# Global attention: values transposed by transposing DMA transfers instead of TensorE transposes and copies

## What is computed

```
def proj(W, bias):
    y = tanh(states @ W + bias)
    return y.reshape(b, s, h, d).transpose(0, 2, 1, 3)
q, k, v = proj(Wq, bq), proj(Wk, bk), proj(Wv, bv)
alpha = einsum('bhqd,bhkd->bhqk', q, k) / sqrt(d)
alpha = softmax(where(causal, alpha, min))
ctx = einsum('bhqk,bhkd->bhqd', alpha, v)
out = tanh(ctx.reshape(b, s, h * d) @ Wo + bo)
```

## Time and profile before

| | us |
|---|---|
| median of 3 runs | 2335.64 (2334.77 to 2335.74) |
| the profiled execution, whole | 2336.77 |
| its span in the profile | 2335.0 |
| PE busy | 2249.1 (96% of the span) |
| DVE busy | 1918.6 (82%) |
| ACT busy | 1510.0 (65%) |
| POOL busy | 525.9 (23%) |
| L785, transposes of values, 512 in all: mean of one | 0.22 |
| L626, copy of the high values, 32 in all: mean of one | 1.02 |
| L338, copy of the low values, 32 in all: mean of one | 0.68 |

### The profile page before, as it was taken

One profiled execution on the slowest core, in us unless ns is written; L12 is line 12 of the kernel. 1 busy time (PEld: TensorE's weight loads), 2 busy tenths in 40 slices (PEclk: granted clock), 3 DMA queues, 4 the chain that ended last, 5 costly groups with the idle time before them and its releaser, 6 DMA issues.

```text
span 2335.0 us, 61234 instructions
## 1 busy us (share of the span) xinstructions
PE 2249.1 (96%) x21120; PEld 1734.1 (74%) x21120; DVE 1918.6 (82%) x4512; ACT 1510.0 (65%) x2969; POOL 525.9 (23%) x637
## 2 busy tenths in 40 slices
PE   6999999999999999889999999999999999998999
PEld 4676777777777767567777777788777777776888
DVE  6999799979998999768888888567588888886776
ACT  5777577757776777447677766444476777765443
POOL 2000000000000000154555554012255555551000
PEclk9999999999999999989999999999999999999999
DMA  3100110001001100210000001000100000001110
GB/s 117 47 13 19 38 40 13 13 31 52 13 13 43 58 13 7 84 58 2 9 0 9 0 9 39 19 1 0 48 1 3 7 4 5 5 5 31 60 36 28
DMA packets 66987, 58.20 MB, mean 25 GB/s; under 512 B 4037, under 2 KB 64317, under 8 KB 66625
## 3 DMA queue, kind: packets, MB, share of 16 engines
q1 hardware_dynamic: 66880, 56.81, 7.9%
HBM read 44.21 MB, written 8.40 MB: 23 GB/s over the span
## 4 chain that ended last, share of the span: by engine, by line
PE 53%; DVE 2%; issue 1%; ACT 1%; POOL 0%; DVEq 0%; POOLq 0%; ACTq 0%
PE ly_ps L74 9%; PE ly_ps L75 9%; PE ly_ps L76 9%; PE ly_ps L1930 6%; PE ly_ps L1909 5%; PE ly_ps L1920 5%; PE ly_ps L1947 5%; PE ly_ps L1901 3%; PE ly_ps L1940 1%; PE ly_ps L1957 1%; PE ly_ps L1985 1%; PE ly_ps L1878 1%; DVE ly_masked L1598 1%; DVE ly_rope_t L1569 0%; DVE ly_rope_a L1566 0%
## 5 line engine op out<-in xcount | busy, mean ns | idle before, releaser
L610 ACT ACTIVATE at_p<-at_ps_s,at_shift 128x1024 f32<-128x1024 f32 (+3 forms) x384 | 335.5, 899 | 89.8 <-PE at_ps_s L814 48.9
L349 DVE TENSOR_TENSOR at_p_lo<-at_p,at_p_hi 128x1024 f16<-128x1024 f32 (+3 forms) x384 | 357.4, 952 | 5.5
L1371 ACT ACTIVATE ly_probs<-ly_masked,ly_small,ly_rq 128x256 f32<-128x256 f32 x512 | 301.6, 594 | 13.8 <-DVE ly_small L1601 13.8
L842 PE MATMUL at_ps_o<-at_v,at_p_hi 128*128 128x65 f16 x2304 | 238.0, 193 | 3.4 <-DVE at_p_lo L349 2.5
L842 PEld LDWEIGHTS at_ps_o<-at_v,at_p_hi 128*128 128x128 f16 x2304 | 210.6, 96 | 38.6 <-issue 25.8
L843 PE MATMUL at_ps_o<-at_v,at_p_hi 128*128 128x64 f16 x2304 | 237.1, 194 | 0.0
L1598 DVE CUSTOM_DVE_ANT_0 ly_masked<-ly_ps,ly_mask 128x256 f32<-128x256 f32 x512 | 196.1, 421 | 49.0 <-PE ly_ps L1909 36.6
L844 PE MATMUL at_ps_o<-at_v,at_p_lo 128*128 128x65 f16 x2304 | 236.0, 192 | 0.0
L1225 POOL TENSOR_TENSOR ly_rope_a<-ly_rope_a,ly_rope_t 128x512 f32<-128x512 f32 x128 | 164.2, 1283 | 318.5 <-DVE ly_rope_t L1569 318.5
L1379 ACT ACTIVATE ly_operands_plain<-ly_ps 128x512 f32<-128x512 f32 x256 | 153.3, 599 | 111.8 <-PE ly_ps L1920 103.9
L344 DVE CAST at_p_hi<-at_p 128x1024 f16<-128x1024 f32 (+3 forms) x384 | 206.8, 557 | 22.3 <-ACT at_p L610 13.5
(11 more groups left out here) (247 smaller groups left out, 6057.6 us busy)
## 6 DMA issues: line engine op xcount, KB each, us to landing
at_w_raw<-in_Wv SPq DMA_DIRECT2D x32, 128.0 KB, 2.3
at_w_raw<-in_Wq SPq DMA_DIRECT2D x32, 128.0 KB, 2.4
at_w_raw<-in_Wk SPq DMA_DIRECT2D x32, 128.0 KB, 2.4
at_xio<-in_states SPq DMA_DIRECT2D x4, 1024.0 KB, 6.7
ly_a_raw<-x SPq DMA_DIRECT2D x8, 512.0 KB, 4.4
out<-stream SPq DMA_DIRECT2D x16, 256.0 KB, 2.3
ly_shifted<-stream SPq DMA_DIRECT2D x8, 508.0 KB
x<-at_xio SPq DMA_DIRECT2D x3, 1024.0 KB, 4.4
```

What stands on the lines that cost most here:

```text
L349: dve.tensor_tensor(p_lo[u % P_RING][:, :, off:], probs[u % P_RING][:, :, off:], p_hi[u % P_RING][:, :, off:], ALU.subtract).then_inc(p_lo ...
L610: act.activation(probs[u % P_RING][:, :, off:], ps_s[u % 2][:, :, off:], ACT.Exp, bias=shift[:], scale=SCORE_SCALE).then_inc(exp_done, 1)
L842: pe.matmul(out, ph, ones_hi, start=(kt == 0 and t == 0), stop=False, skip_group_check=True)
L1371: step = act.activation(pr[:, j % 2, h, :], sm[:, j % 2, h, :], ACT.Exp, bias=small[:, j % 2, 1, h:h + 1], scale=rq[:, par, 2 * j + h:2 * ...
```

## The change

The two parts of `vT` are transposed by three DMA transfers with `transpose=True`, issued by SyncE: one for each head of the high part (64 x 1024), one for the whole low part (128 x 1024). SyncE waits for the second value chunk's low part (`pj_lo`) and issues them behind the weight loads. The value tile is laid out anew: in each tile of 128 keys first the two heads' high values, each with 16 columns of ones behind it (`VS = DH + 16`), then the low values of both. One semaphore, `vt_done`, stands for all three (48 per pair). TensorE's transposes, the copies on ScalarE and VectorE and the waits of the projections 1 to 3 for them go; the first projection of the next pair waits for `vt_done`, since it leads to a write of `vT`, and so do the value products. SyncE's loop over pairs is written out.

```diff
-VW = 2 * DH + 2
+VS = DH + 16
+VW = 2 * VS + 2 * DH
...
+VT = 3 * 16
...
+        def high_values(par):
+
+            return v[par][:, :, 0:2 * VS].rearrange("p t (h c) -> p t h c", h=2)
+
+        def low_values(par):
+
+            return v[par][:, :, 2 * VS:VW]
...
+                def transpose_values(n):
+
+                    sp.wait_ge(pj_lo, at(NPJ * n + NC))
+                    for h in range(2):
+                        sp.dma_start(high_values(n % 2)[:, :, h, 0:DH], vT[0][h * DH:(h + 1) * DH, :],
+                                     transpose=True).then_inc(vt_done, 16)
+                    sp.dma_start(low_values(n % 2), vT[1][:], transpose=True).then_inc(vt_done, 16)
...
                 load_w(1)
+                transpose_values(0)
...
-                    with sp.Fori(0, ahead) as j:
-
-                        hold(sp, tick, (wh_done, at(b * HP + j + 2)), (wl_done, at(b * HP + j + 2)))
-                        load_w(b * HP + j + 2)
+                    for j in range(ahead):
+                        n = b * HP + j + 2
+                        sp.wait_ge(wh_done, at(n))
+                        sp.wait_ge(wl_done, at(n))
+                        load_w(n)
+                        transpose_values(n - 1)
...
                         load_w(b * HP + HP + 1)
+                        transpose_values(b * HP + HP)
                     else:
+                        transpose_values(NPAIR - 1)
...
-                    pool.memset(v[i][:, :, :, DH:DH + 2], 1.0).then_inc(const_done, 1)
+                    pool.memset(high_values(i)[:, :, :, DH:VS], 1.0).then_inc(const_done, 1)
...
-                def low_values(n, dst):
-
-                    dve.wait_ge(vt_mm, 2 * n + 2)
-                    dve.tensor_copy(v[dst][:, :, :, DH + 2:VW], ps_m16[0]).then_inc(vt_lo, 1)
...
-                def high_values(n, dst):
-                    act.wait_ge(vt_mm, 2 * n + 1)
-                    act.activation(v[dst][:, :, :, 0:DH], ps_m16[1], ACT.Copy).then_inc(vt_hi, 1)
...
                     if i == 0:
                         pe.wait_ge(wl_done, at(it + 2))
-                        pe.wait_ge(vt_lo, at(it + 1))
+                        pe.wait_ge(vt_done, VT * it + VT)
                         pe.wait_ge(ct_lo, at(NC * it - 1))
                     elif i == 1:
-                        pe.wait_ge(vt_hi, at(it + 1))
                         pe.wait_ge(ct_lo, at(NC * it))
-                    elif i == 2:
-                        pe.wait_ge(vt_lo, at(it + 2))
-                    elif i == 3:
-                        pe.wait_ge(vt_hi, at(it + 2))
                     else:
...
-                def values(part, base):
-
-                    pe.wait_ge(pj_lo if part else pj_hi, at(base + NC))
-                    for t in range(TB):
-                        step = pe.transpose(ps_m16[1 - part][:, t, :, :].rearrange("p h d -> p (h d)"),
-                                            vT[part][:, t * P:(t + 1) * P], ident16[:])
-                    step.then_inc(vt_mm, 1)
...
                     if u == 0:
-                        pe.wait_ge(vt_hi, at(it + 1))
-                        pe.wait_ge(vt_lo, at(it + 1))
+                        pe.wait_ge(vt_done, VT * it + VT)
...
-                        ones_hi, lo = v[par][:, kt, h, 0:DH + 1], v[par][:, kt, h, DH + 2:VW]
+                        ones_hi, lo = high_values(par)[:, kt, h, 0:DH + 1], low_values(par)[:, kt, h * DH:(h + 1) * DH]
...
-                values(0, 0)
-                values(1, 0)
+                pe.wait_ge(const_done, 3)
...
                         scores(b, it, par, 4, 5)
-                        if ahead_of:
-                            values(0, ahead)
                         value_products(b, it, par, 1)
-                        if ahead_of:
-                            values(1, ahead)
                         value_products(b, it, par, 2)
                         value_products(b, it, par, 3)
```

More of the change, by code:

```diff
@@ L117, in phase_modulation_and_attention @@
         qk = [[keep["qk"][0:2], keep["qk"][2:4]], [keep["qk"][4:6], keep["k1"]]]
-        v = [a.sb(f"at_v{i}", [P, TB, 2, VW], F16) for i in range(2)]
+        v = [a.sb(f"at_v{i}", [P, TB, VW], F16) for i in range(2)]
         probs = [a.sb(f"at_p{i}", [P, 2, CH]) for i in range(P_RING)]
@@ L137, in phase_modulation_and_attention @@
         ps_m = [a.ps(f"at_ps_m{i}", [P, CH]) for i in range(2)]
[L138 to L144, removed]
+        (ld_const, ld_wo, ld_w, ld_x, const_done, wo_done, sc_done, pv_done, pj_mm, vt_done, ct_mm, op_mm, yt_mm,
+         exp_done, pj_full, ct_hi, y_done, p_hi_done, pj_hi, wh_done, p_lo_done, pj_lo, wl_done, r_done, cx_done,
+         ct_lo, yg_done, x1_done, tick) = a.sems(
+            "at_", "ld_const ld_wo ld_w ld_x const_done wo_done sc_done pv_done pj_mm vt_done ct_mm op_mm yt_mm "
+            "exp_done pj_full ct_hi y_done p_hi_done pj_hi wh_done p_lo_done pj_lo wl_done r_done cx_done "
+            "ct_lo yg_done x1_done tick")
         (ld_cond, ld_mod, ld_rows, ld_ident, st_rows, exp_cond, silu_done, mod_mm, mod_ev, row_mm, row_ev,
@@ L270, in _ @@
                         sp.wait_ge(pj_lo, at(NPJ * NPAIR))
-                        sp.wait_ge(vt_mm, 2 * NPAIR)
+                        sp.wait_ge(vt_done, VT * NPAIR)
                         sp.dma_start(rope[:].rearrange("p a t d -> p (a t d)"), io["rope"]).then_inc(keep["ld_rope"], 16)
@@ L319, in _ @@
             def _(dve):
-                for s in (p_hi_done, p_lo_done, pj_lo, wl_done, r_done, cx_done, vt_lo, ct_lo, yg_done, x1_done):
+                for s in (p_hi_done, p_lo_done, pj_lo, wl_done, r_done, cx_done, ct_lo, yg_done, x1_done):
                     dve.sem_inc(s, CREDIT)
@@ L485, in _ @@
                 split_weights(1)
-                dve.wait_ge(const_done, 3)
-                low_values(0, 0)
                 modulation_rows()
@@ L505, in pair @@
                         high_probs(it, 4)
-                        if ahead_of:
-                            low_values(it + 1, dst)
                         reciprocals(it, 0)
@@ L597, in _ @@
             def _(act):
-                for s in (exp_done, pj_full, pj_hi, vt_hi, ct_hi, y_done, wh_done):
+                for s in (exp_done, pj_full, pj_hi, ct_hi, y_done, wh_done):
                     act.sem_inc(s, CREDIT)
@@ L674, in _ @@
                 act.wait_ge(const_done, 3)
-                high_values(0, 0)
                 for b in range(B):
@@ L694, in pair @@
                         exps(it, 6)
-                        if ahead_of:
-                            high_values(it + 1, dst)
                         if ahead_of:
```

## The result

The changed kernel takes 2310.22 us (median of 4, 2308.52 to 2311.35), the one before 2335.27 (2334.77 to 2335.74) on the same chip: ratio 0.989, interval [0.9875, 0.9905], 25.1 us less. I had forecast 2315 us. Copies and transposes are gone from the page, and the hardware queue moves 16.8 MB more than in the earlier trace rows.

A forecast was written before the change was run, and what follows sets the result against it. TensorE was taken to set the pace in attention, VectorE 1.3 us behind. Pairs 18.6 us plus start 1.8 make 20.4 us less, transfers costing nothing: 2316.4 from the profiled execution, predicted 2315 us, range 2304 to 2436.

The forecast's parts named there:

- its own forecast: Whole kernel: 0.45 to 0.75 us gained a pair, giving 2311 to 2321 us; chance 0.42.
- 0.6 us a pair: Attention pairs: of 0.90 us of TensorE transposes removed, 0.6 stays; 31 pairs give 18.6 us (9.3 to 27.9).
- unit 3: Last of three value products before the next scores: due at 555.77, waits for VectorE's low probabilities, starts near 556.1.
- the handover: From VectorE's end of low probabilities to TensorE's waiting value product: some 0.2 us.
- The start, 1.8 us: Before the first scores: 16 more transposes stand in the open; removing them gains 1.8 us (bounds 0.5 and 1.8).
- The transfers hidden: SyncE's queue, each pair: three transfers need 2.3 to 7 us, below the 18.8 before TensorE stands still; no cost.
- the two ways of counting: Transfer cost at 44 ns a packet: 32-byte runs take 45 us, 256-byte pieces 5.6 us.
- Rival (a): Each pair's first projection waits for late transfers, from a chain of 18.8 us on; +100 us, 2436 us; chance 0.28.
- Beyond attention the stretches must be equally long.: Sign for the profile after: from 960 us on, the stretches keep their length.
- (b): Attention pairs: VectorE becomes the bound, holding TensorE at a second place; 0.3 us a pair stay, 2325 us; chance 0.12.
- (c): Attention pairs: the whole 0.90 us stays, 29.7 us less, 2306 us; chance 0.11.
- (d): Transfer chain just over its limit, or crossbar writes hinder engines; gain and loss cancel within 0.2%; chance 0.07.

The follow-up runs named there:

- e1: Changed kernel with TensorE's 16 value transposes per pair put back, results unused, values still by transfers, no copies: 2330.33 us.
- e6: Changed kernel with the ScalarE and VectorE copies out of PSUM put back, without TensorE's transposes: 2310.73 us.
- e2: Changed kernel with only the high part by transfers; low part again by 8 TensorE transposes and the VectorE copy: 2315.47 us.
- e5: Changed kernel with VectorE's subtraction for the second value projection moved behind the high and low probabilities of unit 3: 2301.51 us.
- e11: Changed kernel with the 16 TensorE transposes of the start put back, results unused, none in the pairs: 2309.09 us.
- e3: Changed kernel with each pair's three transfers done twice, the second set after the first landed, TensorE waiting for the last: 2309.71 us.
- e7: Changed kernel with each pair's three transfers done three times, each set after the one before has landed: 2336.88 us.
- e10: Kernel before the change with only the VectorE step moved, unit 3's probabilities ahead of the subtraction for the second value projection: 2341.69 us.

## Why the prediction was right

- **The number.** 2310.2 is 0.8 us outside the 2311 to 2321 that the prediction gave its own forecast, and inside the range only because that reached from 2304 to 2436. The forecast was 20.4 us less; the profiles show 21.7 in attention and its start, as below, and 5.5 behind it.
- **The bound.** TensorE, not VectorE: shown from both sides by e1 (with the transposes alone the pairs are back at 939.4 us) and e6 (nothing comes back with the copies alone). The two windows of the earlier trace rows are not one pair each: a pair took 25.9 to 26.2 us before, not 26.45. The sum does not rest on them.
- **0.6 us a pair.** Measured 0.65. The mechanism is the one written down, unit 3's product against its low probabilities; the handover was 0.06 us in one pair, where I had taken 0.2. The account closes: 31 x 0.90 = 27.9 us were removed, 20.3 came, and unit 3's gaps hold 7.5 of the 7.6 that are missing. e2 shows the first group counting in full, and e5 gives back 6.7 us in the pairs, 0.22 each, so that 0.87 of the 0.90 is then collected.
- **The start, 1.8 us.** The size came near by luck. The profiles show 1.4, but e11 finds no price for the transposes; how long the clock's low level lasts there, which the prediction left out, moves the start as much.
- **The transfers hidden.** Right. A set needs 5.8 us from its first issue to the last landing (I gave 2.3 to 7, and e3's expectation 7, which counted the landing from the end of the issue) against 18.7. The packets confirm the lower figure of the two ways of counting: 68,608 more packets for 16.8 MB are 245 bytes each, not 32, and 13.0% of 16 x 2307.8 us less the 7.9% of before makes 27 ns each. Rival (a) needed three sets to become true, and then in 7 pairs only (e7). Of the Trainium skill's two figures, 1309 ns for a block ("VectorE: DVE Perf Modes", The three transpose paths) would make an estimated 10.5 us of the low part's eight blocks; it landed in 3.2. The other, 261 GB/s, would make an estimated 2 us of the 512 KB; the set took 5.8, of which issuing filled 4.0.
- **"Beyond attention the stretches must be equally long."** This failed, by 5.5 us in the profiles, and it is the main reason why the kernel came out at 2310 and not at 2315. The prediction had put this stretch at nothing; what the clock does in it was not considered, and its cause stays open.
- **Rivals (b), (c), (d).** (b) did not come: unit 3's is the only new wait, and e6 shows that VectorE could still carry the copy at no cost. (c) did not come by itself, since unit 3 held TensorE; e5 brings it. (d) did not come: e1 and e3 show no cost of the transfers above 1 us.

## What to carry to other kernels

Where one engine is dense, follow the removed work to the first consumer that is then too early: here that was one value product, and moving one VectorE step collected the rest. A move that is wrong before a change can be right after it (e5 and e10), so retry orders once a consumer has slack. The transposing transfers were free here because their queue is nearly idle and the data has 18.7 us where a set takes 5.8; three sets one after the other were already too long in some pairs.

## What was not expected of the hardware

Three transposing transfers of 512 KB in all cost SyncE 1.3 to 1.4 us of issue each (plain ones 0.37 to 0.5), landed 2.8 to 3.2 us after the issue began, and did not slow the pairs (918.2 us with one set and with two, e3). The clock of TensorE in an unchanged stretch differed by kernel and was worth 5 us of 2335; a comparison under 0.3% between kernels like these needs the stretches' clocks beside it.
